# First rows in two loads ahead of U3 and the state, and TensorE's first products from a tile that VectorE clears

## The chip, the core and the metric
The kernel runs on one core of a Trainium2 chip. The metric is the device time of one execution in microseconds, and the median of three is compared. TensorE is written PE below, VectorE DVE, ScalarE ACT, GpSimd POOL and SyncE SP.

## The reference
Three steps of a gated graph network on `x` (64 batches, 128 nodes, 256 features), then a residual and a layer norm. Both adjacency operands are the same `adj`, so both halves of `av` are the same.
```python
for _ in range(3):
    a = einsum('nm,bmd->bnd', adj, h); av = concatenate([a, a], -1)
    z = sigmoid(lin(av, w3) + lin(h, u3)); r = sigmoid(lin(av, w4) + lin(h, u3))
    hv = tanh(lin(av, w5) + lin(r * h, u5)); h = (1 - z) * h + z * hv
return layernorm(x + h)
```

## The kernel before
The 64 batches are cut into 16 groups of four (512 rows), and four groups (slots) share a round of twelve frames: a frame is one step of one group. There are four rounds, the middle of the program is a loop over rounds, and everything is written out by hand with semaphores between the engines, each of which works through its own list in order. A product in the frames is three single-pass products of 128x128 weights on 128x512 columns (`hi` and `lo` halves of both operands, `product`, L418 to L420).

The change touches the start of the program alone. There the state of the first group and its weights come straight from memory:

- The ACT queue issues `first_in` (L747: the four batches of the first group with nodes on the partitions, and `adj` transposed, 4608 bytes for each of 128 partitions) and then `lead_in` (L748: U3 and the first feature chunk of the first group's state, 4096 bytes for each partition).
- The SP queue waits for `neg_half_ready`, the last of POOL's start operations, and then issues the state's second chunk (L376, 2048 bytes for each partition), the weights W4 (`wide`, L373), the biases, W5, W3, the second group's rows (L381) and more.
- PE runs `keep_warm(13)` (L549): 13 transposes of the identity tile that POOL makes (L1140, L1142), whose results nothing reads. Then `first_aggregate(0)` (L438: 8 products of 128x128 fp32 on the rows, into `ps_a`), `first_u` (L510, 12 products with U3 on `hT_hi` and `hT_lo`), `first_dense` with W4 (12), with W5 into `ps_v` (12) and with W3 (12), then the second group's aggregate and the frames.
- ACT rounds the state to `hT_hi` (L680, one operation for each chunk), then the aggregate to `aT_hi` (L656), then the summed W4 and W5 to `wt_hi` (L745).
- DVE does in this order: U3's high and low parts (L992, L994), `hT_lo` of chunk 0 (L918), the sum of W4's two halves (L977), `hT_lo` of chunk 1, `aT_lo` twice (L865), W4's low part (L987), three bias sums, the sums of W5 and W3 (L977), and so on.

Of the kernel before, what the change touches and what calls it, by code (L numbers as in the profile page):

```python
# [54 lines left out]
P = 128  # L55
EPS = 1e-5


def build(nc, x_rows, first_rows, second_rows, lead, x_cols, w3_t, w4_t, w5_t, u5_t, biases, out_rows):
    N, B, D = out_rows.shape  # L60
    ROWS = 512
    GB = ROWS // N
    C = D // P
    HB = GB // 2
# [7 lines left out]
    DMA = 16  # L72
# [7 lines left out]
    with ctx:  # L80
        def sb(name, shape, dt=F32):
            return ctx.enter_context(nc.sbuf_tensor(name, shape, dt))

        def ps(name):
            return ctx.enter_context(nc.psum_tensor(name, [P, 2, ROWS], F32))

        def sem(name):
            return ctx.enter_context(nc.semaphore(name))


        ident = sb("ident", [P, P])
        neg_half = sb("neg_half", [P, GB])
        wide = [sb(f"wide{k}", [P, 2, C, D]) for k in range(3)]
        lead_in = sb("lead_in", [P, C * D + C * ROWS])
# [4 lines left out]
        bias = sb("bias", [P, 3, C])  # L99
        wt_hi = [sb(f"wt_hi{k}", [P, C, D], F32R) for k in range(5)]  # L100
        wt_lo = [sb(f"wt_lo{k}", [P, C, D], F32R) for k in range(5)]
        first_in = sb("first_in", [P, GB * D + N])
        adjT = first_in[:, GB * D:GB * D + N]
        W3, W4, W5, U3, U5 = range(5)
        BZ, BR, BV = range(3)

# [16 lines left out]
        aT = sb("aT", [P, QUADS, LINE])  # L123
        z = [sb(f"z{k}", [P, C, ROWS]) for k in range(2)]
        y = [sb(f"y{k}", [P, GB, D]) for k in range(2)]
        x_first = [first_in[:, 0:GB * D].rearrange("p (b d) -> p b d", b=GB), y[1]]
        y_tail = sb("y_tail", [P, GB, D])


# [15 lines left out]
        ps_g = [ps(f"ps_g{k}") for k in range(2)]  # L145
# [8 lines left out]
        def by_chunk(bank):  # L154

            return bank.rearrange("p (c r) -> p c r", c=C)
# [17 lines left out]

        w_loaded = [sem(f"w_loaded{k}") for k in range(5)]
        lead_loaded, bias_loaded = sem("lead_loaded"), sem("bias_loaded")
        ident_zero, ident_ready, neg_half_ready = sem("ident_zero"), sem("ident_ready"), sem("neg_half_ready")
        wsum_ready, bias_ready = sem("wsum_ready"), sem("bias_ready")
        wt_hi_ready, wt_lo_ready = sem("wt_hi_ready"), sem("wt_lo_ready")
# [1 line left out]


        x_loaded = [sem(f"x_loaded{k}") for k in range(2)]
        rows_first = sem("rows_first")
        stored = [sem(f"stored{k}") for k in range(2)]


# [15 lines left out]
        rows_second = sem("rows_second")  # L203
# [34 lines left out]
        def frames(i, j):  # L238

            return FR * i + (j + 1)  # L240
# [58 lines left out]
        def _(sp):  # L299
            def load_cols(i, q):  # L300
                sp.dma_start(xT[q][:, :, :], x_cols[bass.ds(SLOTS * i + q, 1), :, :, :]
                             .rearrange("g p c r -> p (g c) r")).then_inc(xT_loaded[q], DMA)
# [69 lines left out]
            def load_wide(k):  # L372
                sp.dma_start(wide[k][:, :, :, :], wide_in[k]).then_inc(w_loaded[k], DMA)  # L373
# [4 lines left out]
            sp.dma_start(bias_in[:, :, :], biases).then_inc(bias_loaded, DMA)  # L378
            load_wide(W5)
            load_wide(W3)  # L380
            sp.dma_start(x_first[1][:, :, :], second_rows).then_inc(rows_second, DMA)  # L381
            load_cols(0, 1)
            sp.dma_start(square[1][:, :, :], u5_t).then_inc(w_loaded[U5], DMA)
            load_rows(0, 2)
# [30 lines left out]
        def _(pe):  # L415
# [13 lines left out]

            def first_aggregate(j):  # L430

                pe.wait_ge(rows_second if j == 1 else rows_first, DMA)
                for hf in range(2):
                    bank = by_chunk(ps_a[:, hf, :])
                    for bb in range(HB):
                        b = hf * HB + bb
                        for c in range(C):
                            done = nc.tensor.matmul(bank[:, c, bb * N:(bb + 1) * N],  # L438
                                                    x_first[j][:, b, c * P:(c + 1) * P],
                                                    adjT[:, :], start=True, stop=True)  # L440
                    done.then_inc(a_ready, 1)

            def aggregate(i, j, first=False):

                pe.wait_ge(hn_hi_ready, split_aggregates(i, j))
                pe.wait_ge(hn_lo_ready, split_aggregates(i, j))
                if first:
                    pe.wait_ge(adj_lo_ready, 1)
                    pe.wait_ge(a_lo_ready, 2 * frames(0, 1))
                else:  # L450
                    pe.wait_ge(ab_ready, split_aggregates(*frame_before(i, j)))
                for k in range(2):
                    cols = slice(k * ROWS, (k + 1) * ROWS)
                    product(ps_a[:, k, :], adjT_hi[:, :], adjT_lo[:, :], hn_hi[:, cols], hn_lo[:, cols],
                            True, True).then_inc(a_ready, 1)
# [8 lines left out]
            def update_product(i, j, carry):  # L464

                if carry or j >= 2:
                    pe.wait_ge(z_ready, C * frames(*two_before(i, j)))
                u_product(i, j)
# [28 lines left out]
            def candidate(i, j):  # L497

                pe.wait_ge(rh_hi_ready, C * frames(i, j))
                pe.wait_ge(rh_lo_ready, C * frames(i, j))  # L500
                for oc in range(C):
                    dense(ps_v, U5, oc, rh_hi, rh_lo, False, True).then_inc(vpre_ready, 1)

            def weight_ready(k):
                pe.wait_ge(wt_hi_ready, PREPARED.index(k) + 1)
                pe.wait_ge(wt_lo_ready, PREPARED.index(k) + 1)
# [6 lines left out]
            def first_u():  # L513

                pe.wait_ge(u3_hi_ready, 1)
                for kc in range(C):
                    pe.wait_ge(hT_hi_ready, kc + 1)
                    for oc in range(C):
                        part(ps_g[0], wt_hi, U3, oc, kc, hT_hi, kc == 0, False)
                    pe.wait_ge(u3_lo_ready, 1)  # L520
                    for oc in range(C):
                        part(ps_g[0], wt_lo, U3, oc, kc, hT_hi, False, False)
                for kc in range(C):
                    pe.wait_ge(hT_lo_ready, kc + 1)
                    for oc in range(C):
                        part(ps_g[0], wt_hi, U3, oc, kc, hT_lo, False, False)

            def first_dense(dst, k, start, stop, done):

                pe.wait_ge(wt_hi_ready, PREPARED.index(k) + 1)  # L530
                pe.wait_ge(a_hi_ready, 2)
                for kc in range(C):
                    for oc in range(C):
                        part(dst, wt_hi, k, oc, kc, aT_hi, start and kc == 0, False)
                pe.wait_ge(a_lo_ready, 2)
                for kc in range(C):
                    for oc in range(C):
                        part(dst, wt_hi, k, oc, kc, aT_lo, False, False)
                pe.wait_ge(wt_lo_ready, PREPARED.index(k) + 1)
                for oc in range(C):  # L540
                    for kc in range(C):
                        end = part(dst, wt_lo, k, oc, kc, aT_hi, False, stop and kc == C - 1)
                    if done:
                        end.then_inc(done, 1)

            def keep_warm(n):

                for _ in range(n):
                    nc.tensor.transpose(ps_g[0][:, 0, 0:P], ident[:, :], ident[:, :])  # L549

            def first_round():

                pe.wait_ge(ident_ready, 1)
                keep_warm(13)
                first_aggregate(0)
                first_u()
                first_dense(ps_g[0], W4, False, True, rpre_ready)
                first_dense(ps_v, W5, True, False, None)
                pe.wait_ge(r_ready, C)
                first_dense(ps_g[0], W3, False, True, zpre_ready)  # L560
                first_aggregate(1)
                update_product(0, 1, False)
                weight_ready(U5)
                candidate(0, 0)
                aggregate(0, 2, first=True)
                for j in range(1, FR - 2):
                    frame(0, j, False)
                second_half(0, FR - 2, False)
# [50 lines left out]
            def last_part(source, c, start, stop):  # L619
# [4 lines left out]
                                            start=start, stop=stop, skip_group_check=True)  # L624
                return done

            pe.wait_ge(a_lo_ready, 2 * frames(last, FR - 1))
            for c in range(C):
                pe.wait_ge(h_ready, C * frames(last, FR - 2) - 1 + c)
# [23 lines left out]
        def _(act):  # L653
# [91 lines left out]
                nc.scalar.copy(wt_hi[k][:, :, :], weight(k)[:, :, :]).then_inc(wt_hi_ready, 1)  # L745

            act.dma_start(first_in[:, :], first_rows).then_inc(rows_first, DMA)  # L747
            act.dma_start(lead_in[:, 0:C * D + ROWS], lead).then_inc(lead_loaded, DMA)  # L748

            act.wait_ge(neg_half_ready, 1)  # L750
# [19 lines left out]
            j = FR - 1  # L770
# [65 lines left out]
        def _(dve):  # L836
# [151 lines left out]
                                        ALU.subtract).then_inc(wt_lo_ready, 1)  # L988


            dve.wait_ge(lead_loaded, DMA)
            nc.vector.tensor_copy(wt_hi[U3][:, :, :], square[0][:, :, :]).then_inc(u3_hi_ready, 1)  # L992
            dve.wait_ge(u3_hi_ready, 1)
# [27 lines left out]
            j = FR - 1  # L1021
# [181 lines left out]
```

## Time and profile before
| | us |
|---|---|
| median of 3 runs | 735.11 (735.06 to 735.43) |
| profiled execution | 734.97 |
| its span, first to last instruction | 732.9 |
| PE busy in it | 726.1 |
| DVE busy | 635.7 |
| ACT busy | 419.4 |

The profiled execution's own time is 2.07 us above its span; that part lies outside the instructions. "PE busy" counts from a product's start to its modelled end, so it is no measure of the array's rate. In the rows, PEld is the load of weights into PE, an engine name with q is its queue, and the last bracket of a timeline row is the idle time before it and what ended it.

### The profile page before, as it was taken

The page shows a single profiled execution, that of the slowest core. Times are in us where ns is not written, and L with a number is a line of the kernel's source. Part 1 is how long each engine was busy: PE and PEld are TensorE (multiplying, and loading weights), DVE is VectorE, ACT ScalarE, POOL GpSimd, SP SyncE. Part 2 cuts the span into 40 slices and gives each one's busy share as a digit, 9 for nine tenths or more (in the row PEclk, how much of TensorE's full clock was granted, in tenths as well). Part 3 has the DMA queues.
Part 4 walks back from the last instruction along what each step waited for, and adds up shares of the span by engine and source line. Part 5 has one row for each costly group of instructions (what it writes and reads, how often), then busy time and mean ns, then how long its engine had stood idle before and what let it go on. Part 6 is the DMA issues. An engine that isn't in the chain of part 4 may idle for free.

```text
span 732.9 us, 9687 instructions
## 1 busy us (share of the span) xinstructions
PE 726.1 (99%) x3237; PEld 602.3 (82%) x3237; DVE 635.7 (87%) x932; ACT 419.4 (57%) x647; POOL 29.9 (4%) x71
## 2 busy tenths in 40 slices
PE   9999999999999999999999999999999999999997
PEld 7888888888888888888888888888888888888886
DVE  6788898889998888898999888899899987899887
ACT  5645655465666654565566754565556664565546
POOL 0000000000010000000011000000011000000013
PEclk9999999999999999999999999999999999999999
DMA  8145454446766445445567445544467544544442
GB/s 345 61 145 168 136 184 143 140 148 186 237 225 194 160 148 172 152 137 167 188 237 229 156 139 172 184 140 134 163 203 254 195 159 143 164 132 134 142 145 116
DMA packets 74183, 124.13 MB, mean 169 GB/s; under 512 B 8368, under 2 KB 55472, under 8 KB 74160
## 3 DMA queue, kind: packets, MB, share of 16 engines
q1 hardware_dynamic: 72144, 116.43, 48.8%
q10 hardware_dynamic: 2016, 7.41, 2.8%
q8 instruction: 13, 0.21, 0.1%
q14 instruction: 10, 0.08, 0.0%
HBM read 67.18 MB, written 56.62 MB: 169 GB/s over the span
## 4 chain that ended last, share of the span: by engine, by line
PE 98%; DVE 1%; ACT 0%; issue 0%; POOLq 0%; POOL 0%; DVEq 0%
PE ps_g L420 17%; PE ps_g L418 17%; PE ps_g L419 17%; PE ps_v L420 12%; PE ps_v L418 12%; PE ps_v L419 12%; PE ps_a L420 3%; PE ps_a L418 3%; PE ps_a L419 3%; PE ps_g L510 1%; PE ps_a L438 1%; PE ps_g L549 0%; PE ps_v L510 0%; DVE dz L1072 0%; DVE stats L1037 0%
## 5 line engine op out<-in xcount | busy, mean ns | idle before, releaser
L685 ACT ACTIVATE ps_v<-ps_v,bias 128x512 f32<-128x512 f32 x94 | 62.2, 662 | 182.7 <-PE ps_v L420 182.7
L418 PE MATMUL ps_g<-aT_hi,wt_lo 128*128 128x512 f32 (+1 forms) x380 | 147.1, 387 | 0.0
L420 PE MATMUL ps_g<-aT_hi,wt_hi 128*128 128x512 f32 (+1 forms) x380 | 147.0, 387 | 0.0
L419 PE MATMUL ps_g<-aT_lo,wt_hi 128*128 128x512 f32 (+1 forms) x380 | 147.0, 387 | 0.0
L724 ACT ACTIVATE z<-ps_g,bias 128x512 f32<-128x512 f32 x94 | 64.8, 690 | 95.0 <-PE ps_g L420 94.6
L418 PEld LDWEIGHTS ps_g<-aT_hi,wt_lo 128*128 128x128 f32 x380 | 71.3, 188 | 14.6
L419 PEld LDWEIGHTS ps_g<-aT_lo,wt_hi 128*128 128x128 f32 x380 | 71.3, 188 | 14.5
L420 PEld LDWEIGHTS ps_g<-aT_hi,wt_hi 128*128 128x128 f32 x380 | 71.3, 188 | 14.5
L870 DVE TENSOR_TENSOR aT_lo<-aT,aT_hi 128x1024 fp32r<-128x1024 f32 x46 | 56.4, 1225 | 30.4 <-ACT aT_hi L660 30.4
L860 DVE STREAM_TRANSPOSE ab<-ps_a 128x1024 f32<-128x1024 f32 x46 | 57.4, 1249 | 23.5 <-PE ps_a L420 22.3
L418 PE MATMUL ps_v<-rh_hi,wt_lo 128*128 128x512 f32 x192 | 74.7, 389 | 0.0
L419 PE MATMUL ps_v<-rh_lo,wt_hi 128*128 128x512 f32 x192 | 74.7, 389 | 0.0
L420 PE MATMUL ps_v<-rh_hi,wt_hi 128*128 128x512 f32 x192 | 74.7, 389 | 0.0
L708 ACT ACTIVATE r_sb<-ps_g,bias 128x512 f32<-128x512 f32 x94 | 64.9, 690 | 16.3 <-PE ps_g L420 16.3
L418 PE MATMUL ps_v<-aT_hi,wt_lo 128*128 128x512 f32 x188 | 73.2, 389 | 0.0
L418 PE MATMUL ps_g<-hT_hi,wt_lo 128*128 128x512 f32 x188 | 73.2, 389 | 0.0
L419 PE MATMUL ps_g<-hT_lo,wt_hi 128*128 128x512 f32 x188 | 73.1, 389 | 0.0
L419 PE MATMUL ps_v<-aT_lo,wt_hi 128*128 128x512 f32 x188 | 73.1, 389 | 0.0
L420 PE MATMUL ps_g<-hT_hi,wt_hi 128*128 128x512 f32 x188 | 73.1, 389 | 0.0
L420 PE MATMUL ps_v<-aT_hi,wt_hi 128*128 128x512 f32 x188 | 73.1, 389 | 0.0
L892 DVE TENSOR_TENSOR dz<-dz,z 128x512 f32<-128x512 f32 x94 | 64.7, 688 | 1.6
L912 DVE TENSOR_TENSOR rh_lo<-rh,rh_hi 128x512 fp32r<-128x512 f32 x96 | 61.8, 684 | 0.3 <-ACT rh_hi L799 0.2
(126 smaller groups left out, 1237.0 us busy)
## 6 DMA issues: line engine op xcount, KB each, us to landing
turned_a<-ab SPq DMA_DIRECT2D x46, 512.0 KB, 3.7
aT<-turned_a SPq DMA_DIRECT2D x184, 128.0 KB, 3.0
turned_h<-hb SPq DMA_DIRECT2D x46, 512.0 KB, 2.6
hn<-turned_h SPq DMA_DIRECT2D x184, 128.0 KB, 3.0
x_in<-in_x_rows SPq DMA_DIRECT2D x14, 512.0 KB, 4.6
xT<-in_x_cols SPq DMA_DIRECT2D x12, 512.0 KB, 4.3
out<-y ACTq DMA_DIRECT2D x12, 512.0 KB, 3.6
wide<-in_w_t SPq DMA_DIRECT2D x3, 512.0 KB, 6.6
```

The costliest lines, as they stand in the source:

```text
L418: nc.tensor.matmul(dst, lhs_lo, rhs_hi, start=first, stop=False, skip_group_check=True)
L419: nc.tensor.matmul(dst, lhs_hi, rhs_lo, start=False, stop=False, skip_group_check=True)
L420: return nc.tensor.matmul(dst, lhs_hi, rhs_hi, start=False, stop=last, skip_group_check=True)
L438: done = nc.tensor.matmul(bank[:, c, bb * N:(bb + 1) * N], x_first[j][:, b, c * P:(c + 1) * P], adjT[:, :], start=True, stop=True)
L510: return nc.tensor.matmul(dst[:, oc, :], w[k][:, kc, oc * P:(oc + 1) * P], state[:, kc, :], start=start, stop=stop, skip_group_check=True)
L685: nc.scalar.activation(ps_v[:, oc, :], ps_v[:, oc, :], ACT.Tanh, bias=bias[:, BV, oc:oc + 1]).then_inc(v_ready, 1)
L708: nc.scalar.activation(r_sb[:, oc, :], ps_g[j % 2][:, oc, :], ACT.Sigmoid, bias=bias[:, BR, oc:oc + 1]).then_inc(r_ready, 1)
L724: nc.scalar.activation(z[j % 2][:, oc, :], ps_g[j % 2][:, oc, :], ACT.Sigmoid, bias=bias[:, BZ, oc:oc + 1]).then_inc(z_ready, 1)
L860: nc.vector.transpose(ab[:, :, :].rearrange("p q x -> p (q x)"), ps_a[:, :, :].rearrange("p k x -> p (k x)")).then_inc(ab_ready, 1)
L870: nc.vector.tensor_tensor(quads_first(aT_lo), by_block(aT), f32(quads_first(aT_hi)), ALU.subtract).then_inc(a_lo_ready, 2)
L892: nc.vector.tensor_tensor(dz[:, c, :], dz[:, c, :], z[j % 2][:, c, :], ALU.mult).then_inc(zd_ready, 1)
L912: nc.vector.tensor_tensor(rh_lo[:, c, :], rh[:, c, :], f32(rh_hi[:, c, :]), ALU.subtract).then_inc(rh_lo_ready, 1)
```

## The change
The load `first_in` is cut in two. The first now holds two of the four batches and `adj` transposed (2560 bytes for each partition), the second the two other batches (2048 bytes), which go into half of `y[0]`, a buffer of the output stage. Both stand in the ACT queue ahead of `lead_in`. PE's wait for the rows is split, half by half. The 13 transposes become 6 ordinary fp32 products of a zero tile `warm`, which DVE clears as its first operation. PE's wait for the identity moves to the end of the program, ahead of the first transpose that reads it.
```diff
-        first_in = sb("first_in", [P, GB * D + N])
-        adjT = first_in[:, GB * D:GB * D + N]
+        first_in = sb("first_in", [P, HB * D + N])
+        adjT = first_in[:, HB * D:HB * D + N]
...
             def first_aggregate(j):
 
-                pe.wait_ge(rows_second if j == 1 else rows_first, DMA)
                 for hf in range(2):
+                    if j == 0:
+                        pe.wait_ge((rows_first, rows_rest)[hf], DMA)
+                    elif hf == 0:
+                        pe.wait_ge(rows_second, DMA)
...
             def keep_warm(n):
 
                 for _ in range(n):
-                    nc.tensor.transpose(ps_g[0][:, 0, 0:P], ident[:, :], ident[:, :])
+                    nc.tensor.matmul(ps_g[0][:, 0, 0:P], warm[:, :], warm[:, :], start=True, stop=True)
 
             def first_round():
 
-                pe.wait_ge(ident_ready, 1)
-                keep_warm(13)
+                pe.wait_ge(warm_ready, 1)
+                keep_warm(6)
...
             act.dma_start(first_in[:, :], first_rows).then_inc(rows_first, DMA)
+            act.dma_start(y[0][:, HB:GB, :], first_rest).then_inc(rows_rest, DMA)
             act.dma_start(lead_in[:, 0:C * D + ROWS], lead).then_inc(lead_loaded, DMA)
...
+            nc.vector.memset(warm[:, :], 0.0).then_inc(warm_ready, 1)
             dve.wait_ge(lead_loaded, DMA)
```
ACT's list from the start of the program, before:
```order
L747 DMA first_in<-in_first_rows 128x1152
L748 DMA lead_in<-in_lead 128x1024
L751 ACT_TABLE_LOAD
L751 ACTIVATE table_probe<-neg_half 128x4
L680 CAST hT_hi<-lead_in 128x512 x2
L656 CAST aT_hi<-ps_a 128x2x256 x2
```
and after the change:
```order
L757 DMA first_in<-in_first_rows 128x640
L758 DMA y<-in_first_rest 128x512
L759 DMA lead_in<-in_lead 128x1024
L762 ACT_TABLE_LOAD
L762 ACTIVATE table_probe<-neg_half 128x4
L690 CAST hT_hi<-lead_in 128x512 x2
L666 CAST aT_hi<-ps_a 128x2x256 x2
```
One transfer more stands ahead of `lead_in`; the casts that follow keep their order. SP's list is the same in both.

PE's list from the start of the program, before:
```order
L549 MATMUL ps_g<-ident 128x128 x13
L438 MATMUL ps_a<-first_in 128x128 x8
L510 MATMUL ps_g<-hT_hi,wt_hi 128x512 x2
L510 MATMUL ps_g<-hT_hi,wt_lo 128x512 x2
L510 MATMUL ps_g<-hT_hi,wt_hi 128x512 x2
L510 MATMUL ps_g<-hT_hi,wt_lo 128x512 x2
```
and after the change:
```order
L558 MATMUL ps_g<-warm 128x128 x6
L447 MATMUL ps_a<-first_in 128x128 x4
L447 MATMUL ps_a<-first_in,y 128x128 x4
L519 MATMUL ps_g<-hT_hi,wt_hi 128x512 x2
L519 MATMUL ps_g<-hT_hi,wt_lo 128x512 x2
L519 MATMUL ps_g<-hT_hi,wt_hi 128x512 x2
```
Six instructions stand where 13 stood, the eight products of the aggregate are the same in two groups of four, and nothing behind them moves. DVE has one row more, the clearing of `warm`, as its first.

## Rows read from the trace of the kernel before

**Rows 1.** All engines by stretch: us, busy (count) per engine, PEclk, DMA share, GB/s
```profile
core 0: us, PE busy (x) PEld busy (x) DVE busy (x) ACT busy (x) POOL busy (x), PEclk, DMA share, GB/s
...
7.08:12.58 5.50, 5.50 (x25) 4.28 (x25) 5.20 (x12) 2.47 (x5) 0.00 (x0) 1.00 0.97 384
...
19.90:722.60 702.70, 702.70 (x3106) 581.94 (x3106) 616.49 (x889) 402.06 (x615) 27.14 (x59) 1.00 0.51 165
...
722.60:732.90 10.30, 5.03 (x40) 4.54 (x39) 6.92 (x22) 6.20 (x13) 2.04 (x6) 0.99 0.37 148
```

**Rows 2.** The chain that ended last, 0 to 20 us: start, us, what
```profile
1.52 3.03 PE ps_g L549 x13
...
4.55 2.52 PE ps_a L438 x16
...
7.08 5.51 PE ps_g L510 x24
...
12.58 2.81 PE ps_v L510 x12
...
18.11 1.78 PE ps_a L438 x16
```

**Rows 3.** Timeline, 0 to 8 us, queues and POOL: start, us, engine, line, tiles
```profile
0.73 0.40 ACTq L747 DMA_DIRECT2D first_in<-in_first_rows  x1
...
0.73 0.20 POOL L1140 MEMSET ident<- 128x128 f32 x1 [0.29 <-POOLq L1193]
...
1.16 0.45 ACTq L748 DMA_DIRECT2D lead_in<-in_lead  x1
...
1.55 0.39 SPq L376 DMA_DIRECT2D lead_in<-in_x_cols  x1
...
1.99 0.43 SPq L373 DMA_DIRECT2D wide<-in_w_t  x1
```

**Rows 4.** DMA issues, 0 to 30 us: count, KB each, us to landing
```profile
first_in<-in_first_rows ACTq DMA_DIRECT2D x1, 576.0 KB, 3.7
...
lead_in<-in_lead ACTq DMA_DIRECT2D x1, 512.0 KB, 4.6
...
lead_in<-in_x_cols SPq DMA_DIRECT2D x1, 256.0 KB, 4.9
```

**Rows 5.** Landing of the three loads into `wide`, from its tile's view
```profile
DMA to landing us min/median/max: 5.8/6.6/7.3
```

**Rows 6.** DMA queues of the stretch 1.5 to 4.6 us
```profile
q10 hardware_dynamic: 245, 1.00, 90.8%
```

**Rows 7.** All engines by stretch; DMA share and GB/s stand last
```profile
5.00:6.00 1.00, 1.00 (x8) 1.00 (x8) 0.20 (x1) 0.20 (x1) 0.00 (x0) 1.00 0.93 293
...
6.00:7.00 1.00, 1.00 (x11) 1.00 (x10) 0.96 (x3) 0.95 (x3) 0.00 (x0) 1.00 1.00 399
```

**Rows 8.** Timeline, 5.79 to 12.6 us: ACT, DVE and PE's weight loads
```profile
5.79 1.28 ACT L680 CAST hT_hi<-lead_in 128x512 fp32r<-128x512 f32 x2 [2.66 <-DMA lead_in<-in_lead]
...
5.80 0.43 DVE L992 CAST wt_hi<-lead_in 128x512 fp32r<-128x512 f32 x1 [5.80 <-DMA lead_in<-in_lead]
...
6.26 0.69 DVE L994 TENSOR_TENSOR wt_lo<-lead_in,wt_hi 128x512 fp32r<-128x512 f32 x1
...
6.87 0.68 DVE L918 TENSOR_TENSOR hT_lo<-lead_in,hT_hi 128x512 fp32r<-128x512 f32 x1
...
7.77 0.69 DVE L977 TENSOR_TENSOR wsum<-wide 128x512 f32<-128x512 f32 x1 [0.21 <-DMA wide<-in_w_t]
...
10.99 1.29 DVE L977 TENSOR_TENSOR wsum<-wide 128x512 f32<-128x512 f32 x2
...
11.71 0.62 ACT L745 CAST wt_hi<-wsum 128x512 fp32r<-128x512 f32 x1 [2.60 <-DVE wsum L977]
...
12.38 0.77 PEld L510 LDWEIGHTS ps_v<-aT_hi,wt_hi 128*128 128x128 f32 x4 [0.22 <-ACT wt_hi L745]
```

**Rows 9.** Line 438 by stretch: PE busy, weight loads, PEclk, DMA share, GB/s
```profile
4.50:5.30 0.80, 0.79 (x3) 0.79 (x4) 1.00 0.92 330
...
6.10:6.90 0.80, 0.80 (x9) 0.78 (x8) 1.00 1.05 420
```

**Rows 10.** Timeline, 20 us: a DVE operation on a tile of 128x128
```profile
20.11 0.28 DVE L953 TENSOR_TENSOR adjT_lo<-first_in,adjT_hi 128x128 fp32r<-128x128 f32 x1
```

More of the change, by code:

```diff
@@ L56, with build @@
 EPS = 1e-5
-def build(nc, x_rows, first_rows, second_rows, lead, x_cols, w3_t, w4_t, w5_t, u5_t, biases, out_rows):
+def build(nc, x_rows, first_rows, first_rest, second_rows, lead, x_cols, w3_t, w4_t, w5_t, u5_t, biases, out_rows):
     N, B, D = out_rows.shape
@@ L91, in build @@
         ident = sb("ident", [P, P])
+        warm = sb("warm", [P, P])
         neg_half = sb("neg_half", [P, GB])
@@ L125, in build, with x_first @@
         y = [sb(f"y{k}", [P, GB, D]) for k in range(2)]
-        x_first = [first_in[:, 0:GB * D].rearrange("p (b d) -> p b d", b=GB), y[1]]
+        def x_first(j, b, cols):
+            if j == 0 and b < HB:
+                return first_in[:, b * D + cols.start:b * D + cols.stop]
+            return y[j][:, b, cols]
         y_tail = sb("y_tail", [P, GB, D])
@@ L176, in build @@
         lead_loaded, bias_loaded = sem("lead_loaded"), sem("bias_loaded")
+        warm_ready = sem("warm_ready")
         ident_zero, ident_ready, neg_half_ready = sem("ident_zero"), sem("ident_ready"), sem("neg_half_ready")
@@ L183, in build @@
         x_loaded = [sem(f"x_loaded{k}") for k in range(2)]
-        rows_first = sem("rows_first")
+        rows_first, rows_rest = sem("rows_first"), sem("rows_rest")
         stored = [sem(f"stored{k}") for k in range(2)]
@@ L380, in _ @@
             load_wide(W3)
-            sp.dma_start(x_first[1][:, :, :], second_rows).then_inc(rows_second, DMA)
+            sp.dma_start(y[1][:, :, :], second_rows).then_inc(rows_second, DMA)
             load_cols(0, 1)
@@ L438, in first_aggregate @@
                             done = nc.tensor.matmul(bank[:, c, bb * N:(bb + 1) * N],
-                                                    x_first[j][:, b, c * P:(c + 1) * P],
+                                                    x_first(j, b, slice(c * P, (c + 1) * P)),
                                                     adjT[:, :], start=True, stop=True)
@@ L625, in last_part @@
                 return done
+            pe.wait_ge(ident_ready, 1)
             pe.wait_ge(a_lo_ready, 2 * frames(last, FR - 1))
@@ L1181 @@
         "x_rows": x.reshape(B // GB, GB, N, C, QUADS, BLK).transpose(0, 2, 4, 3, 1, 5).reshape(B // GB, N, GB * D),
-        "first_rows": np.concatenate([x[0:GB].transpose(1, 0, 2).reshape(N, GB * D), adj.T], axis=1),
+        "first_rows": np.concatenate([x[0:GB // 2].transpose(1, 0, 2).reshape(N, GB * D // 2), adj.T], axis=1),
+        "first_rest": x[GB // 2:GB].transpose(1, 0, 2),
         "second_rows": x[GB:2 * GB].transpose(1, 0, 2),
```

## The prediction
> **What bounds the kernel now.** I read the table by stretch first. From 19.9 to 722.6 us PE is busy for all of 702.70 us, and of the last 10.3 us for half [rows 1]. The diff touches neither stretch, except for one wait at the end on an event of the first microseconds. So all that the change can do lies in the first 20 us: what matters is at what time PE gets through its list there, since whatever is gained or lost by then is carried unchanged behind it.
>
> The chain of waits gives these 20 us as PE alone: 13 transposes from 1.52 us, the aggregate from 4.55, 24 products into `ps_g` from 7.08, 12 into `ps_v` from 12.58, and the second aggregate at 18.11 [rows 2]. That reads as if PE were the bound from 1.52 us on. The timeline says otherwise. PE's weight load for the first `ps_v` product starts at 12.38, after 0.22 us of idle that ACT's cast of W5 ended [rows 8]. That cast waited 2.60 us for DVE's sum of W5 (0.65 us, first of the two that start at 10.99). DVE was busy 5.20 of the 5.50 us from 7.08 to 12.58 [rows 1] and works in order, back to its sum of W4 at 7.77, which waited 0.21 us for the transfer of W4 (issued at 1.99, the shortest of the three landings of 5.8 us [rows 3, 5]). Ahead of that stand three operations that start when `lead_in` lands: 5.80, 6.26, 6.87, the last done at 7.55 [rows 8]. The chain that sets 12.38 is therefore transfers, then DVE: **W4 landed at 7.77, or `lead_in` landed at 5.80 plus 1.75 us, whichever is later; now W4, by 0.22.** Behind 12.58 PE is gapless by the chain [rows 2]. An aggregate that is done earlier feeds `aT_hi`, which stands on ACT behind the two casts of the state, and these wait for `lead_in` as well [rows 8].
>
> **PE's own part.** The clearing of `warm` has no row before. A POOL clear of the same size takes 0.20 us, a DVE operation on 128x128 with two inputs 0.28 [rows 3, 10]. DVE can begin about when POOL and ACT begin, 0.73, so PE begins at about 1.0 and not 1.52. The 13 transposes made 13 records in 3.03 us, 0.23 each; an ordinary fp32 product of this size makes two records (8 products, x16) [rows 2]. Six are thus 12 records, 2.8 us, done near 3.8 us (bounds 3.6 and 3.9). The half load of rows is 256 KB shorter than one that landed 3.7 us after issue at 0.73 [rows 3, 4], that is 0.66 us earlier at 399 GB/s [rows 7]: 3.8 us. The 16 records of the aggregate take 2.52 us at the old mix of clocks [rows 2], so they end at 6.3 to 6.5 and not 7.07. This is the gain meant. Its worth is nothing unless `first_u` can start then, and that needs `hT_hi`, `lead_in`'s landing plus one cast (0.62, a half of the 1.28 pair with its overlap) [rows 8]: 6.42 if `lead_in` lands as before. Even then the sum of W4 holds DVE until 7.77, and the 0.6 us reappear as idle ahead of the `ps_v` products. **PE's part: 0.**
>
> **The transfers.** Two things move.
>
> *Order.* `lead_in` was issued at 1.16, now behind one issue more: ACT's issues last 0.40 and 0.45 us [rows 3], so it goes out at about 1.6. SP's second chunk (`lead_in<-in_x_cols`) goes out at 1.55, which POOL sets and nothing changes. Up to now the ACT transfers were ahead, and the queues show what that means: from 1.5 to 4.6 us only ACT's q10 moved anything, 1.00 MB, though SP had issued at 1.55 and 1.99 [rows 3, 6]. Transfers are served nearly in the order of issue. If SP's chunk now goes ahead of `lead_in` or is mixed with it, `lead_in` lands when both are done, which before was the landing of the chunk, 1.55 + 4.9 = 6.45 [rows 3, 4]. That is 0.66 later than 5.79. DVE's three operations then end at 6.46 + 1.75 = 8.21, and the sum of W4 starts there: **+0.44**, after 0.22 of slack. Lower bound 0, if ACT's transfer stays ahead.
>
> The Trainium skill ("DMA: Bandwidth & Descriptors", section on queues, rings and completion order) has each DMA engine alternate between the queues that have work, packet by packet. In this trace q1 moved nothing until 4.6 us. By the page's rule 128 packets of 4 KB against 128 of 2 KB would end together, the same 6.45.
>
> *Size of the packets.* The rows came in packets of 4608 bytes and now come in 2560 and 2048. In 5 to 6 us, where most packets are the 2048-byte ones of SP's chunk, 293 GB/s moved at a busy share of 0.93; in 6 to 7 us, with the 4096-byte ones of W4, 399 at 1.00 [rows 7]. So a 2048-byte packet holds an engine for 2048 x 16 / 315 GB/s = 0.104 us and a 4096-byte one for 0.164: a line with 0.044 us a packet that doesn't depend on size. The change makes 128 packets more, eight on each of 16 engines: 8 x 0.044 = 0.35 us later for everything behind, W4 too. Lower bound 0, if the sparse first microsecond of the transfers hides it; I take 0.3.
>
> The Trainium skill (same page, Specifications) puts the size from which a transfer runs at full rate at 512 bytes. By that rule this term is 0 and the sum would be +0.44; the 293 against 399 above speaks against it, although the chunk's stretch also holds the change from one queue to the other.
>
> **The sum.** `lead_in` lands at 6.45 + 0.3 = 6.75, DVE starts the sum of W4 at 8.50 (W4 itself lands at 7.77 + 0.3 = 8.07), 0.73 later than before, and the first `ps_v` product starts 0.73 later. PE's side of it: `hT_hi` at 7.37, 24 products in 5.5 us, 12.9; so the cast of W5 at 13.1 still ends last. Nothing of this comes back, since PE is gapless later. **+0.7 us**: 734.97 + 0.7 = 735.7 for the profiled execution; against the median, which is 0.14 above it, 735.8. A difference within 0.2% (1.47 us) can't be told from no change.
>
> **The rivals.**
> - *`lead_in` stays ahead of SP's chunk* (ACT's second and third issue go out quickly, or ACT's queue has precedence). For it: q10 alone moved until 4.6 us. Then only the packets count: `lead_in` 6.1, its operations done at 7.85, W4 at 8.07, **+0.3**, 735.4.
> - *A small gain.* As above and the small packets are free: W4 lands at 7.77 or, with `lead_in` slightly earlier, is no later; DVE could win at most the 0.21 us that it waited if W4 too came earlier. **0 to -0.2**, 734.9 to 735.1. Against it: the bytes ahead of W4 are the same 1.9 MB. The split and the earlier PE would then do nothing that the time shows.
> - *Slower, by the clock.* PE's granted clock reads 1.00 throughout, yet four weight loads lie in 0.80 us from 4.5 and eight in 0.80 us from 6.1 [rows 9]: the same work at the lower level (1.2 GHz) and then at the higher (2.4 GHz), with the rise about 4 us after PE's start at 1.52. Now PE is idle from 6.4 to about 7.4, and the warm-up is of zeros. If the rise came only 4 to 4.5 us after 7.4, the products until 11.6 would run at half speed: 4.2 / 2 = 2.1 us lost, less the 0.25 by which the W5 cast comes later than PE: 1.85 more, **+2.5**, 737.6. It decides from a rise later than 7.9. For it: nothing in the trace shows a low clock after so short a gap; against it: PE worked from 1.52 with only a 0.4 us gap and rose during the aggregate, and now it works from 1.0 to 6.4.
> - *The change doesn't start PE earlier* (PE isn't ready at 1.0): then PE's list shifts by 0.5 us and is hidden by the same wait for DVE, so the sum stays.
>
> **How the numbers follow.** Forecast 54%, `lead_in` ahead 27%, small gain 13%, clock 6%. The forecast's own range is +0.44 to +0.8. The range goes from the small gain (734.9) to the forecast's upper bound (735.9), widened by the spread of the runs shown (0.05 down, 0.32 up): 734.8 to 736.3; the clock case is left out. Slower by over 0.2% is most of the clock case, 4%; faster by over 0.2% has no mechanism here, 1%; within 0.2% 95%.
>
> **What the profile after would show.** PE's first product at about 1.0 and 12 records of it; the aggregate from about 3.8 to 6.4; `lead_in` issued at 1.6 and DVE's cast of U3 at 6.75 (6.1 in the first rival); idle of PE ahead of L519 of nearly 1 us; DVE's sum of W4 at 8.5 with no wait for `wide`; the `ps_v` products at 13.1 to 13.3; from there the same list, 0.7 later. What would make it wrong: a DVE cast at 5.8 or earlier, a second low stretch of PE's clock, or an effect in the loop, which the order of the transfers can't cause.

## The result: 4.1 us slower
| | before | after |
|---|---|---|
| median, us | 735.17 (735.06 to 735.66) | 739.32 (738.17 to 739.83) |
| ratio | | 1.0051, 95% interval 1.0041 to 1.0062 |
| profiled execution, us | 734.97 | 739.55 |
| its span, us | 732.9 | 737.5 |

The forecast was 735.8 in a range from 734.8 to 736.3, "within 0.2%" at 95%. The median is 4.15 us longer, 0.5 to 0.6%, and outside the range.

The chain of waits of the changed kernel, 0 to 32 us; its lines answer to [rows 2]:
```profile
1.65 7.16 DMA lead_in<-in_lead
...
8.83 0.63 ACT hT_hi L690
...
9.59 7.33 PE ps_g L519 x24
...
16.92 2.72 PE ps_v L519 x12
...
22.36 1.78 PE ps_a L447 x16
```
Before, this stretch was PE alone. Now the chain begins with the flight of `lead_in`, 7.16 us where 4.6 was the landing before [rows 4]. The 24 products into `ps_g` start at 9.59 instead of 7.08, which is 2.51 us, and take 7.33 us instead of 5.51, 1.82 more. The `ps_v` products take 0.09 less, since PE no longer waits ahead of them. The second aggregate takes 1.78 as before and is followed by the frames at 24.14 instead of 19.90: 2.51 + 1.82 - 0.09 = 4.24.

All engines by stretch, in the columns of [rows 1]:
```profile
core 0: us, PE busy (x) PEld busy (x) DVE busy (x) ACT busy (x) POOL busy (x), PEclk, DMA share, GB/s
...
9.59:13.00 3.41, 3.41 (x9) 2.58 (x10) 3.41 (x7) 1.97 (x4) 0.00 (x0) 0.53 1.01 414
...
24.14:726.84 702.70, 702.70 (x3107) 581.93 (x3106) 616.50 (x889) 402.48 (x615) 27.22 (x59) 1.00 0.51 165
...
726.84:737.50 10.66, 5.13 (x40) 4.55 (x39) 7.03 (x22) 6.21 (x13) 2.05 (x6) 0.97 0.35 143
```
The granted clock is 0.53 from 9.59 to 13.00 us: the lower level (1.2 GHz). The middle stretch is 702.70 us long, to the hundredth what it was [rows 1]. The tail is 10.66 us where it was 10.30. So 4.24 at the start and 0.36 at the end make the 4.6 us of the span, and nothing happens between them.

The start in the timeline; the lines answer to [rows 3, 8]:
```profile
0.83 0.17 DVE L1002 MEMSET warm<- 128x128 f32 x1 [0.83 <-PEq L1206]
...
1.05 2.93 PE L558 MATMUL ps_g<-warm 128*128 128x128 f32 x12 [1.05 <-DVE warm L1002]
...
1.65 0.45 ACTq L759 DMA_DIRECT2D lead_in<-in_lead  x1
...
3.77 1.99 PE L447 MATMUL ps_a<-first_in 128*128 128x128 f32 x8
...
5.56 1.46 PE L447 MATMUL ps_a<-first_in,y 128*128 128x128 f32 x8
...
8.83 0.43 DVE L1004 CAST wt_hi<-lead_in 128x512 fp32r<-128x512 f32 x1 [7.83 <-DMA lead_in<-in_lead]
...
9.59 1.01 PE L519 MATMUL ps_g<-hT_hi,wt_hi 128*128 128x512 f32 x2 [2.58 <-ACT hT_hi L690]
...
10.50 0.69 DVE L988 TENSOR_TENSOR wsum<-wide 128x512 f32<-128x512 f32 x1
```
The early start works: DVE clears the tile in 0.17 us, PE starts at 1.05, makes 12 records in 2.93 us and begins the aggregate at 3.77 instead of 4.51. But the aggregate ends at 7.02, only 0.05 us earlier than before. Its 16 records take 3.25 us instead of 2.56, since in this execution the granted clock rose to 2.4 GHz at 6.39 us and before at 5.62. And `lead_in`, issued at 1.65, releases DVE at 8.83 and not at 5.80, and PE stands still for 2.58 us ahead of `first_u`. DVE's sum of W4 at 10.50 waits for nothing: W4 isn't last any more.

The transfers, answering to [rows 4], and one stretch of the queues:
```profile
lead_in<-in_lead ACTq DMA_DIRECT2D x1, 512.0 KB, 7.2
...
y<-in_first_rest ACTq DMA_DIRECT2D x1, 256.0 KB, 3.2
...
lead_in<-in_x_cols SPq DMA_DIRECT2D x1, 256.0 KB, 6.7
```
```profile
DMA packets 38, 0.07 MB, mean 169 GB/s; under 512 B 5, under 2 KB 5, under 8 KB 38
...
q1 hardware_dynamic: 33, 0.06, 60.0%
...
q10 hardware_dynamic: 5, 0.00, 3.0%
```
Before, the mean from 3.6 to 4.8 us was 397 GB/s; in these 0.4 us it is 169, with the engines busy at 0.63. The first half of the rows had landed (0.74 + 2.9) and the engines had too little to do, although five transfers had been issued by 2.00 us.

### The profile page after: what moved, and what is told of

Its sections match the earlier page's. It is cut to its first block, busy times and chain, and to the rows that moved or that the text cites. A ratio compares the mean times of both kernels' runs of the same rounds, so it can differ in the third digit from the quotient of the medians.

```text
span 737.5 us, 9687 instructions
## 1 busy us (share of the span) xinstructions
PE 728.3 (99%) x3236; PEld 604.4 (82%) x3236; DVE 635.9 (86%) x933; ACT 419.7 (57%) x647; POOL 30.0 (4%) x71
## 4 chain that ended last, share of the span: by engine, by line
PE 97%; DMA 1%; DVE 1%; ACT 0%; issue 0%; ACTq 0%; POOLq 0%; POOL 0%; DVEq 0%
PE ps_g L424 17%; PE ps_g L425 17%; PE ps_g L426 17%; PE ps_v L425 12%; PE ps_v L424 12%; PE ps_v L426 12%; PE ps_a L425 3%; PE ps_a L424 3%; PE ps_a L426 3%; PE ps_g L519 1%; DMA lead_in<-in_lead 1%; PE ps_v L519 0%; PE ps_a L447 0%; DVE dz L1084 0%; DVE stats L1049 0%
```

## The experiments
Each was timed in rounds with the kernel before on the same chip. The medians of before were 735.18 to 735.36 us.

**Which half of the change?** `split_only` takes the changed kernel and puts the old warm-up back:
```diff
-                pe.wait_ge(warm_ready, 1)
-                keep_warm(6)
+                pe.wait_ge(ident_ready, 1)
+                keep_warm(13)
...
-            nc.vector.memset(warm[:, :], 0.0).then_inc(warm_ready, 1)
```


> The changed kernel with the 13 identity transposes of the kernel before and without the cleared tile; only the rows' load stays cut in two. Theory A (the split alone delays lead_in, by about 3 us, and PE then idles and its clock falls): lead_in lands near 8.8 us, time 739 +- 0.7, as the changed kernel. Theory B (the new warm-up is what loses the clock, its zero products or its early start): lead_in still at 8.8 but no low clock behind 9.6, so 737.5. If the delay of lead_in comes from the earlier start of PE, which I don't believe: 735.1.

Measured: 737.74 us (736.50 to 738.74), ratio 1.0033 (1.0021 to 1.0046). Its chain:
```profile
1.65 6.29 DMA lead_in<-in_lead
...
8.72 5.74 PE ps_g L519 x24
```
`lead_in` is late again (7.95 in this execution), and PE starts `first_u` at 8.72. In the profiled execution the clock held, 5.74 us for the 24 products. The six times lie in two groups, 736.5 to 736.9 and 738.6 to 738.7. The distance is about the 1.8 us of a low clock, but only an execution of the lower group has a profile. So the split alone costs 1.2 to 3.4 us. Theory A's 739 with its 0.7 either way holds three of the six times, theory B's 737.5 none, and the median lies between the groups.

`warm_only` is the kernel before with the cleared tile and the 6 products, and the rows in one load:
```diff
-                pe.wait_ge(ident_ready, 1)
-                keep_warm(13)
+                pe.wait_ge(warm_ready, 1)
+                keep_warm(6)
...
+            nc.vector.memset(warm[:, :], 0.0).then_inc(warm_ready, 1)
```


> The kernel before with the one load of 4608-byte rows, and only the warm-up changed: DVE clears a tile, PE makes 6 zero products from 1.05 us. Theory A (all of the loss is in the transfers): lead_in at 5.8, rows at 4.43, PE idle 0.4 to 0.5 us ahead of the rows, time 735.1 +- 0.3. Theory B (zero products warm PE less): the clock rises later than 5.5, part of the 24 products into ps_g runs at the low level, 736 to 737.

Measured: 735.50 us (735.33 to 737.60), ratio 1.0008 (0.9999 to 1.0018). Six of ten runs were at 735.3 to 735.5, four at 736.8 to 737.6. The profiled execution is one of the four (the first row from the timeline, the second from the chain):
```profile
4.56 3.78 PE L440 MATMUL ps_a<-first_in 128*128 128x128 f32 x16 [0.59 <-DMA first_in<-in_first_rows]
...
8.34 6.17 PE ps_g L512 x24
```
The aggregate takes 3.78 us instead of 2.56 and the next 24 products 6.17 instead of 5.51: the clock rose late, at 9.71 us. PE had stood idle for 0.59 us ahead of the rows. The cleared tile alone is nearly free in the median, but four of its ten runs pay 1.5 to 2.3 us.

`warm_8` is `warm_only` with `keep_warm(8)`, which closes that gap.

> The kernel before with the new warm-up, with 8 zero products instead of 6, 16 records that reach from 1.05 to about 4.7 us, past the landing of the rows at 4.5. The version with 6 ended at 3.9, left PE idle for 0.6 us, and its runs fell in two groups, 735.4 and 737.2, the aggregate at the low clock in the latter. Theory C (the idle time of PE ahead of the rows puts off the rise of the clock in some runs): no run above 736, median 735.4 to 735.7. Rival (where the rise falls is chance with any warm-up that starts at 1.05, or zero products count less): two groups again.

Measured: 735.49 us (735.44 to 736.06), no group above. Zero products warm PE as well as the transposes did when they reach to the rows. That it was the gap rests on ten runs with it and ten without, and the rise moves by itself as well: see `clear_only` below.

**Was it PE's idle time that cost the clock?** `filler` puts 12 more products of the cleared tile ahead of `first_u`:
```diff
                 first_aggregate(0)
+                keep_warm(12)
                 first_u()
```


> The changed kernel with 12 more zero products of the cleared tile between the aggregate and first_u, 24 records or 2.6 us at the high clock, to fill PE's idle time while lead_in is on its way. Theory A (PE's idle time of 2.6 us is what made the clock fall, worth 1.8 us): the 24 products into ps_g take 5.5 and not 7.3 us, time 739.3 - 1.8 = 737.5, and still 2.4 above before because of lead_in. Rival (the clock falls for another reason, or zero products don't hold it): 739 or, if the filler runs past lead_in's landing, 739.5.

Measured: 740.34 us (740.14 to 742.78), ratio 1.0076. By the time alone the theory had failed. The profile says why not (a row of its chain, and one of its waits):
```profile
9.41 5.49 PE ps_g L519 x24
...
PE ps_v L424 <- issue: 2.6, 1, 2.6
```
The 24 products took 5.49 us, the clock held. But PE waited 2.62 us near the end of the program, at 710 us, for nothing but its own next instruction; neither profile shown so far has that. In this execution `lead_in` released DVE at 7.33 already, and it was the filler's own end that kept `first_u` until 9.41. `filler_wide` does the same with three instructions:
```diff
+                for _ in range(3):
+                    nc.tensor.matmul(ps_g[0][:, 0, :], warm[:, :], first_in[:, 0:ROWS], start=True, stop=True)
```


> The changed kernel with PE's idle time filled by three fp32 products of 512 columns (2.6 us at the high clock, results not read), only three instructions more, in place of the twelve small ones, whose run had 2.6 us of idle near the end that belongs to the length of PE's list. Theory A (idle PE lets the clock fall, worth 1.8 us): products into ps_g in 5.5 us, time 739.3 - 1.8 = 737.5. Rival (the fall of the clock isn't from idleness): 739.3 or more.

Measured: 737.84 us (737.07 to 738.21), ratio 1.0029. Its chain:
```profile
9.65 5.77 PE ps_g L519 x24
```
`lead_in` landed as late as in the changed kernel (8.86), but the products took 5.77 us instead of 7.33. Time and profile agree: 1.5 us come back when PE is kept busy until shortly before. The idle time was the cause of the low clock. A gap doesn't always bring it: the profiled execution of `split_only` had 1.20 us of idle at the same place and kept its clock.

The changed kernel, `split_only`, `filler` and `filler_wide` issue the same transfers at the same times, and `lead_in` landed at 8.8, 7.95, 7.3 and 8.9 us in their profiled executions. A landing read from one execution can thus be 1.5 us off from another's.

**Why is `lead_in` late?** `sp_later` lets SP issue its first transfer only when ACT has issued `lead_in`:
```diff
             sp.wait_ge(neg_half_ready, 1)
+            sp.wait_ge(lead_issued, 1)
...
             act.dma_start(lead_in[:, 0:C * D + ROWS], lead).then_inc(lead_loaded, DMA)
+            act.sem_inc(lead_issued, 1)
```


> The changed kernel with one wait more: SP issues its first transfer only once ACT has issued lead_in, about 2.1 us instead of 1.55. Theory A (lead_in is late because SP's chunk and W4 were issued beside it and share the engines with it): lead_in lands at 5.8 to 6.2, PE idles under 1 us, no low clock, time 735.1 to 735.8. Rival P (the shorter packets or the third issue themselves slow ACT's queue): lead_in lands at 7 or later and the time stays above 737.

Measured: 737.17 us (736.70 to 737.29), ratio 1.0023. A row of its DMA issues and one of its chain:
```profile
lead_in<-in_lead ACTq DMA_DIRECT2D x1, 512.0 KB, 4.5
...
2.67 6.26 DMA wide<-in_w_t
```
`lead_in` lands at 6.14, with three transfers on ACT and the same packets. So nearly all of its 3.0 us, 2.7, are the order of issue. But the time didn't come back. Theory A had it at 735.8 or less; rival P had it above 737, but with `lead_in` at 7 or later. SP's chunk is now issued at 2.23 and W4 at 2.67, and W4 lands at 8.93 and is last in the chain, 1.1 us later than before. It was issued 0.68 later, so a part of this can be the later issue.

`bias_on_act` makes no split at all. It moves the biases' 5 KB into ACT's queue between the kernel's own two loads:
```diff
             load_wide(W4)
-            sp.dma_start(bias_in[:, :, :], biases).then_inc(bias_loaded, DMA)
...
             act.dma_start(first_in[:, :], first_rows).then_inc(rows_first, DMA)
+            act.dma_start(bias_in[:, :, :], biases).then_inc(bias_loaded, DMA)
             act.dma_start(lead_in[:, 0:C * D + ROWS], lead).then_inc(lead_loaded, DMA)
```


> The kernel before with the biases' load (5 KB) moved from SP's queue to ACT's, between the rows and lead_in: one issue more ahead of lead_in, with almost no bytes. Theory A (it is the third issue, at 1.65 instead of 1.17 and behind SP's first, that makes lead_in late): SP's chunk starts to move before 4 us, lead_in lands at 6.5 to 8, time 736.5 to 738.5. Theory P (bytes and packets): lead_in within 0.2 us of 5.8, time 735.3.

Measured: 739.00 us (737.62 to 740.57), ratio 1.0049 (1.0034 to 1.0064). DMA issues, the landing of `wide`, and a row of its chain:
```profile
lead_in<-in_lead ACTq DMA_DIRECT2D x1, 512.0 KB, 7.2
...
bias_in<-in_biases ACTq DMA_DIRECT2D x1, 5.0 KB, 3.2
...
DMA to landing us min/median/max: 7.4/8.2/9.0
...
9.64 7.10 PE ps_g L509 x24
```
5 KB do all that the change does: `lead_in` 7.2 us after issue, then a low clock (7.10 us for the 24 products). W4, issued at 1.99 as before, lands at 9.4 instead of 7.8, so here no later issue explains it. The cause is one more transfer ahead of `lead_in`, which puts its issue behind SP's first, not its bytes.

`half_packets` tests the packets: one issue, two runs of 2304 bytes for each partition.
```diff
-            act.dma_start(first_in[:, :], first_rows).then_inc(rows_first, DMA)
+            act.dma_start(first_in[:, :].rearrange("p (h x) -> p h x", h=2),
+                          first_rows.rearrange("h p x -> p h x")).then_inc(rows_first, DMA)
```


> The kernel before with the same two ACT transfers, but the rows' one load laid out in memory so that it moves in two runs of 2304 bytes for each partition instead of one of 4608. One issue, twice the packets. Theory P (packets, the step of the prediction, 0.044 us each on an engine): 8 more on each engine, everything behind the rows lands 0.35 us later, W4 too, time +0.3. Theory A (only the place of the issue matters): landings as before within 0.1, time 735.3.

Measured: 735.25 us (735.18 to 735.36), ratio 1.0000 (0.9991 to 1.0010). DMA issues and the landing of `wide`:
```profile
first_in<-in_first_rows ACTq DMA_DIRECT2D x1, 576.0 KB, 3.6
...
lead_in<-in_lead ACTq DMA_DIRECT2D x1, 512.0 KB, 4.8
...
DMA to landing us min/median/max: 6.1/6.9/7.6
```
The profiled execution shows `lead_in` 0.2 and W4 0.3 us later; the medians differ by 0.07. The term of the prediction exists at most as a few tenths that the time doesn't show. The packets' own records in the kernel before say the same: 84 ns at the median for 2048 bytes and 159 for 4096 (means 96 and 169 on SP's queue). That leaves 9 ns a packet that don't depend on size (23 by the means), not 44, and 0.1 to 0.2 us for eight packets more on each engine.

`sp_early` removes SP's wait for POOL, so that SP issues at 0.87 and ACT's list is untouched.
```diff
-            sp.wait_ge(neg_half_ready, 1)
```


> The kernel before with SP's wait for POOL taken away, so that SP issues its chunk at about 0.75, the three weights from 1.2, and ACT issues as before (0.73, 1.17). Theory A (what is issued beside or ahead of lead_in on the other queue shares the engines with it, whatever the number of issues on ACT): rows and lead_in both land later, rows after 5, lead_in after 7, time 736.5 to 740, while the chunk lands before 4.5. Rival (a third issue on ACT's queue is the cause): lead_in at 5.8 as before, time 735.2 or less, since W4 lands earlier.

Measured: 737.10 us (736.36 to 737.75), ratio 1.0024. DMA issues:
```profile
first_in<-in_first_rows ACTq DMA_DIRECT2D x1, 576.0 KB, 4.3
...
lead_in<-in_lead ACTq DMA_DIRECT2D x1, 512.0 KB, 6.3
```
With only two transfers on ACT both land later, the rows at 5.0 and `lead_in` at 7.5. SP's chunk, issued ahead of `lead_in`, is enough: it is the order over both queues, not the third place in ACT's.

**Does a transfer cost something by itself?** `bias_first` moves the biases to the head of SP's list, behind the issue of `lead_in`:
```diff
             sp.wait_ge(neg_half_ready, 1)
+            sp.dma_start(bias_in[:, :, :], biases).then_inc(bias_loaded, DMA)
             sp.dma_start(xT[0][:, 1, :], x_cols[0, :, 1, :]).then_inc(xT_first[1], DMA)
             load_wide(W4)
-            sp.dma_start(bias_in[:, :, :], biases).then_inc(bias_loaded, DMA)
```


> The kernel before with the biases' 5 KB transfer moved, on SP's own queue, from behind W4 to ahead of the chunk: lead_in (issued at 1.17) stays ahead of all of SP's, and W4 has one transfer more ahead of it, with no bytes to speak of. Theory F (each transfer takes about 0.9 us to be served, whatever its size, and the engines run dry behind a small one): lead_in at 5.8 still, W4 lands 0.9 to 1.3 later than 7.8, DVE's sum of W4 at 8.7 to 9, time 736 to 736.5. Rival M (only the mixing of the queues at lead_in costs): W4 within 0.2 of 7.8, 735.3.

Measured: 736.16 us (735.84 to 736.67), ratio 1.0010 (1.0000 to 1.0019). A row of the DMA issues and one of the timeline:
```profile
lead_in<-in_lead ACTq DMA_DIRECT2D x1, 512.0 KB, 4.7
...
8.92 0.69 DVE L977 TENSOR_TENSOR wsum<-wide 128x512 f32<-128x512 f32 x1 [1.30 <-DMA wide<-in_w_t]
```
`lead_in` is on time, and W4 comes 8.92 - 7.77 = 1.15 us later behind 5 KB; the median is 0.86 longer. W4 is issued at 2.47 instead of 1.99 here, which can be a part of it. In `bias_on_act` its issue didn't move and it came 1.6 later. The 128 packets of 40 bytes take 11 ns each at the median by their records, under 0.1 us for each engine, so it isn't their own time. A transfer more ahead of another costs it one to one and a half microseconds here, with 5 KB or 256 KB in it.

**Versions without the loss.** `rest_on_sp` gives the second half of the rows to SP as its first transfer, with 10 transposes:
```diff
+            sp.dma_start(y[0][:, HB:GB, :], first_rest).then_inc(rows_rest, DMA)
             sp.dma_start(xT[0][:, 1, :], x_cols[0, :, 1, :]).then_inc(xT_first[1], DMA)
...
-            act.dma_start(y[0][:, HB:GB, :], first_rest).then_inc(rows_rest, DMA)
```


> The split kept, but the second half of the rows is SP's first transfer, so that ACT issues two, as before, and lead_in at 1.17 has 256 KB less ahead of it; the warm-up is 10 identity transposes, no tile is cleared. Theory A: first half lands at 3.8, lead_in at 5.1 to 5.4, second half by 6, W4 at 7.8 as before; PE begins first_u at 6.0 to 6.5 but DVE waits for W4, time 735.2 (-0.3 to +0.1). If two transfers on ACT aren't enough to keep lead_in early: above 736.

Measured: 737.95 us (737.33 to 738.42). Its chain:
```profile
2.47 6.52 DMA wide<-in_w_t
```
`lead_in` is early (1.16 + 4.0), but W4, issued at 2.47, lands at 8.99: again one transfer more ahead of it. `rest_on_sp_swap`, with DVE's low part of the second chunk ahead of the sum of W4:

> The version before with one exchange on DVE: the low part of the state's second chunk ahead of the sum of W4, where DVE would wait for W4's landing. Theory A: DVE's chain behind W4 is 0.6 us shorter, PE begins the products into ps_v at 11.9 to 12.1 instead of 12.58, time 734.6 to 734.9. Rival (the second chunk's cast comes too late to fit in): 735.2.

Measured: 737.26 us (736.66 to 738.64), so the expectations of both were wrong. Its profiled execution, the slowest of the ten, had the second half of the rows at 6.25 and 6.54 us for the 24 products. `rest_in_lead` keeps the number of transfers: the second half rides inside `lead_in` (768 KB).
```diff
-            act.dma_start(y[0][:, HB:GB, :], first_rest).then_inc(rows_rest, DMA)
-            act.dma_start(lead_in[:, 0:C * D + ROWS], lead).then_inc(lead_loaded, DMA)
+            act.dma_start(lead_in[:, 0:HB * D + C * D + ROWS], lead).then_inc(lead_loaded, DMA)
```


> The rows' load still cut in two, but the second half rides in lead_in's transfer, so that the transfers and bytes ahead of W4 are those of the kernel before; 10 identity transposes, no cleared tile. Theory F (the number of transfers decides): first half lands at 3.8, lead_in at 5.8, W4 at 7.8; PE begins first_u near 6.5, DVE still waits for W4, time 735.2 (-0.3 to +0.3). If the split itself costs: above 736.

> The version before with DVE's low part of the state's second chunk ahead of its sum of W4. DVE is free at 7.55 and waits for W4 until 7.77; the exchange puts 0.6 us of work there, so the sum of W4 is 0.4 later but what stands behind both is 0.2 earlier. Theory: 735.0 (-0.3 to +0.2). A gain of more than 0.3 or a loss would speak for PE, not DVE, being what waits.

Measured: 736.69 us (735.53 to 738.32) and, with the exchange on DVE, 736.49 us (734.97 to 737.09). `lead_in` landed at 5.8 in both, and the second aggregate began at 18.28 and 17.93 us, against 18.11 before. The start was level; the loss was elsewhere, as this row of PE's timeline in the second shows:
```profile
714.65 0.50 PE L427 MATMUL ps_g<-aT_lo,wt_hi 128*128 128x512 f32 x1 [1.09 <-issue]
```
The same wait for an instruction as in `filler`, 1.09 us here. It stands in the profiles of all four kernels with 10 transposes and no more, 0.8 to 1.1 us, `rest_on_sp` among them. `swap_13` adds three small transposes, so that PE's list is as long as before:
```diff
                 keep_warm(10)
+                for _ in range(3):
+                    nc.tensor.transpose(ps_g[0][0:32, 0, 0:32], ident[0:32, 0:32], ident[0:32, 0:32])
```


> rest_in_lead_swap with three transposes of 32x32 behind the ten, so that PE's list is as long as in the kernel before. If the idle time of PE near 714 us, which the profile puts down to issue, belongs to the length of the list: it is gone, the head stays 0.0 to 0.2 us shorter than before, and the time is 735.0 to 735.3 with some runs higher where the clock rises late. If it belongs to something else in these kernels: 736.2 to 736.6 as without them.

Measured: 734.96 us (734.72 to 735.29, 11 runs) against 735.33 (734.98 to 735.80), ratio 0.9996 (0.9987 to 1.0005). Its chain:
```profile
7.10 5.50 PE ps_g L521 x24
...
12.60 2.72 PE ps_v L521 x12
...
18.04 1.78 PE ps_a L449 x16
```
The wait for the instruction is gone. It doesn't simply grow or shrink with the list: the changed kernel (6 instructions of warm-up as written), `warm_8` (8) and `filler_wide` (9) don't have it either. The split that doesn't add a transfer costs nothing and may give a few tenths, though the interval contains no change.

**The tail.** `clear_only` is the kernel before with DVE's clearing of a tile that nothing reads.
```diff
+            nc.vector.memset(warm[:, :], 0.0).then_inc(warm_ready, 1)
             dve.wait_ge(lead_loaded, DMA)
```


> The kernel before with one operation more: DVE clears a 128x128 tile first, and nothing reads it. The profiles with that operation all have 0.29 us of idle on DVE ahead of the first product with z behind the last tanh, and those without it have none. If the one instruction more in DVE's list causes it: that gap is there, the start is untouched, time +0.3 to +0.4, 735.7. If the gap comes from something else in the changed kernels: no gap, 735.3.

Measured: 735.53 us (735.42 to 736.03) against 735.18 (735.00 to 735.64), ratio 1.0005 (0.9996 to 1.0015). A row of DVE's timeline in it, and its counterpart in the changed kernel:
```profile
725.03 0.42 DVE L1075 TENSOR_TENSOR dz<-dz,z 128x256 f32<-128x256 f32 x1 [0.30 <-DVE dz L1069]
```
```profile
728.54 0.43 DVE L1084 TENSOR_TENSOR dz<-dz,z 128x256 f32<-128x256 f32 x1 [0.29 <-DVE dz L1078]
```
Before, this product followed without idle time. One instruction more at the head of DVE's list gives 0.3 us of idle at 725. The idle stands in the profiles of `filler_wide` and `warm_8` too, which have the instruction, and not in those of `split_only`, `sp_early`, `bias_first` and `swap_13`, which don't. The medians differ by 0.35, about the 0.36 of the changed kernel's tail, though the interval is wider than the effect.

The profiled execution of `clear_only` shows another thing. It is the slowest of its ten (736.03), and this row of its chain says why:
```profile
4.56 3.39 PE ps_a L440 x16
```
PE's list and its transfers are those of the kernel before, PE isn't idle, and yet the aggregate takes 3.39 us instead of 2.52: the clock rose at 7.44 us, not at 5.62. So the time of the rise varies without any gap. The second aggregate starts 0.75 us later by it, and a start of the program that looks that much longer or shorter in one profile may be no more than this.

## Why the prediction was wrong, by its steps
- **PE's own part: right in its worth, not in its steps.** It was put at a start of 1.0, an end of the warm-up between 3.6 and 3.9 and a worth of 0; the records show 1.05 and 3.98. The aggregate was to end at 6.3 to 6.5, "at the old mix of clocks"; it ended at 7.02, since the clock rose later. `warm_8`, without the split, is 0.3 us slower, which is the tail.
- **The order of the transfers: the step that failed first.** "`lead_in` lands when both are done", the chunk's old landing, was a term of +0.66 in that landing, worth +0.44. It landed 3.0 us later, and the 2.51 us by which `first_u` starts late are this. I took the engines' time by bytes, held W4 to be behind and the engines to be full. But `lead_in` shared the engines with W4 too, and the engines ran half empty from 4.0 to 4.4 us. `sp_later` shows this step in isolation: `lead_in` back at 6.1. The Trainium skill's rule that the engines alternate between queues ("DMA: Bandwidth & Descriptors", queues, rings and completion order) stood in the prediction against the fact that q1 moved nothing until 4.6 us. In the changed kernel both queues move in each stretch from 3.6 to 8.8 us, so the trace agrees with it as far as both take turns. It doesn't show the even turns of single rows that the prediction made of it: from 6.8 to 7.2 us q1 moved 37 packets and q10 seven. By the page a packet is a group of descriptors, typically 9 to 17; the prediction took the profile's packets for it, one row of one partition each.
- **The size of the packets: the cause was wrong, and the term too small.** I laid 293 against 399 GB/s to the 2048-byte packets. The same bytes in half as long packets in one issue give the same time (`half_packets`), and the packets' own records leave 9 ns that don't depend on size, not 44. What does put W4 off is one transfer more. The 293 GB/s would then belong to transfers too small to cover the time of serving the next; that reading is argued. The Trainium skill's 512 bytes for the full rate (same page, Specifications), which the prediction set aside, agrees with `half_packets`, whose packets are all above it. In cost, 0.3 was put down where the runs show 1.15 (`bias_first`) to 1.7 (the changed kernel: W4 at 2.00 + 7.5 instead of 7.79). The "1.9 MB ahead of W4" in the rival of the small gain are the bytes with W4 itself; ahead of it are 1.4.
- **The clock: right mechanism, wrong chance.** The rival put the break at a rise later than 7.9 us and its price at half the low stretch. The low stretch ran to 13.2 us, and the price was 1.8 us. It had 6% and was left out of the range, because the idle time of PE was forecast at 1.0 us. (The "0.4 us gap" early in PE's work that stands against it there isn't in the trace: PE is busy from 1.52 on.) It became 2.6 us through the order of the transfers. The low clock was there in the profiled execution and, by the mean granted clock of each run (0.997 in five of six, 0.999 in the run of 738.17), in most of the others. `filler_wide` shows this step in isolation.
- **"One wait at the end on an event of the first microseconds" as all that touches the rest: wrong by 0.36 us.** The profile shows no time spent in that wait. DVE's one operation more brings 0.3 us of idle in the tail, and `clear_only`, which has the operation and not the wait, shows it too.
- **The sum.** 2.51 (transfers) + 1.82 (clock) - 0.09 + 0.36 (tail) = 4.60 us for the profiled execution, where +0.7 was forecast.

What stays open: what it is that costs a microsecond or more for each transfer. The runs show it for 5 KB and for 256 KB, on either queue, but no run varies the number of packets of a small transfer. It isn't a late start of what follows: W4's first packet moved at 5.52 us before, at 5.71 in `bias_first` and at 5.75 in the changed kernel. Its last packets are what came late, and the records don't say on which engine. Nor is the wait of PE at 710 to 714 us explained beyond that it comes and goes with the number of instructions in its list.

## What to carry to other kernels
At the start of a program, count transfers and not only bytes: a load cut in two, or a 5 KB load ahead of a needed one, can cost that one over a microsecond. Write down the issue times of all queues in one list and read who stands ahead of whom: here `lead_in`, issued 0.1 us behind the first transfer of the other queue instead of 0.4 ahead of it, landed 3.0 us later. And where PE may run dry at the start, price a low clock behind it: a gap of 2.6 us cost another 1.8. Take a landing or a rise of the clock from several executions where you can: here both moved by over a microsecond between kernels with the same start.

## What was not expected of the hardware
- One transfer of 5 KB (128 packets of 40 bytes) more ahead of a 512 KB one put its landing off by 1.15 us (`bias_first`, issued 0.48 us later as well) and by 1.6 us (`bias_on_act`, issued at the same time). From 4.0 to 4.4 us in the changed kernel the 16 engines moved 169 GB/s with five transfers issued and not all landed.
- PE's clock rose at different times in executions in which PE had no gap over 0.1 us until then: at 4.49 us in `filler_wide`, 5.62 before, 6.90 in `split_only`, 7.44 in `clear_only`. With a gap of 0.59 us it rose at 9.71 in `warm_only`, of which four runs in ten took 736.8 to 737.6 and six 735.3 to 735.5.
- The number of instructions in an engine's list decides waits for its own instructions 700 us later: on PE none with 13 written ones of warm-up and filler, 0.8 to 1.1 us with 10, none with 6, 8 or 9, 2.62 us with 18; on DVE 0.3 us with one operation more.
